# Slots of the timetable set anew in a relative-position attention layer with a ternary feed-forward

## The reference

```python
idx = clip(r[None, :] - r[:, None], -64, 64) + 64
h = layernorm(x)
q, k, v = proj(h, Wq, bq), proj(h, Wk, bk), proj(h, Wv, bv)          # (8, 16, 1024, 16)
logits = einsum('bhqd,bhkd->bhqk', q, k) + einsum('bhqd,qkd->bhqk', q, embK[idx])
w = softmax(logits)
out = einsum('bhqk,bhkd->bhqd', w, v) + einsum('bhqk,qkd->bhqd', w, embV[idx])
x = x + layernorm(out.reshape(8, 1024, 256) @ Wo.T + bo)
delta = 0.7 * mean(abs(Wf))
Wt = where(Wf > delta, 1, where(Wf < -delta, -1, 0)) * alpha
x = x + layernorm(layernorm(x) @ Wt.T + bf)
```

## Time and profile before

| | |
|---|---|
| median of 3 runs | 2754.64 us (2754.41 to 2755.69) |
| the profiled execution | 2754.83 us |
| its span, first to last instruction | 2753.0 us |
| mean granted clock of PE | 0.98 of 2.4 GHz |
| busy: PE, DVE, ACT, POOL | 94%, 74%, 56%, 35% |
| transfers | 409.11 MB, mean 149 GB/s |

### The profile page before, as it was taken

How to read it: one execution, slowest core, us unless ns; L and a number is a source line. 1 busy time by engine, 2 the same in 40 slices (tenths; PEclk the granted TensorE clock), 3 DMA queues, 4 the chain that set the end, 5 groups by cost and what they waited for, 6 DMA issues and landing times.

```text
span 2753.0 us, 102969 instructions
## 1 busy us (share of the span) xinstructions
PE 2594.8 (94%) x43410; PEld 1969.1 (72%) x43410; DVE 2033.1 (74%) x5187; ACT 1552.1 (56%) x2993; POOL 956.8 (35%) x2275
## 2 busy tenths in 40 slices
PE   5899999999999999999999999999999999999995
PEld 3577777677777777767777777767777677777773
DVE  3777678777886778866788667877678766887775
ACT  2455566556565555555555565555665556566651
POOL 3114323433344333443244332444323433341026
PEclk8799999999999999999999999999999999999997
DMA  7656655456455564555645556446655457445410
GB/s 220 182 140 181 166 150 144 121 168 190 126 153 136 154 181 139 143 147 156 173 129 155 160 156 168 131 127 180 169 150 141 115 169 195 137 137 152 131 43 28
DMA packets 605048, 409.11 MB, mean 149 GB/s; under 512 B 149162, under 2 KB 604330, under 8 KB 604330
## 3 DMA queue, kind: packets, MB, share of 16 engines
q1 hardware_dynamic: 604586, 402.54, 51.7%
HBM read 206.84 MB, written 194.90 MB: 146 GB/s over the span
## 4 chain that ended last, share of the span: by engine, by line
PE 70%; DVE 15%; issue 4%; POOL 4%; ACT 3%; SPq 1%; DMA 1%; DVEq 0%; POOLq 0%; ACTq 0%
PE oacc L797 16%; PE logitsT L759 15%; PE scores L736 15%; PE logitsT L764 7%; DVE maxes L1016 6%; DVE junk L1013 6%; PE misc L860 4%; PE misc L693 4%; ACT wxr L1216 2%; PE misc L822 2%; POOL rs L1249 2%; PE misc L710 2%; PE misc L810 2%; PE misc L834 2%; POOL rs L1254 1%
## 5 line engine op out<-in xcount | busy, mean ns | idle before, releaser
L1013 DVE CUSTOM_DVE_ANT_1 junk<-scores,bands 128x512 bf16<-128x512 f32 x988 | 679.1, 687 | 490.8 <-PE scores L736 470.5
L759 PE MATMUL logitsT<-qs,ks 98*128 98x128 bf16 (+3 forms) x9088 | 995.0, 216 | 21.5 <-ACT wxr L1216 12.4
L1216 ACT ACTIVATE wxr<-logitsT 128x512 f32<-128x512 f32 x1024 | 588.6, 603 | 527.6 <-PE logitsT L759 437.5
L759 PEld LDWEIGHTS logitsT<-qs,ks 98*128 98x128 bf16 (+1 forms) x9088 | 678.7, 99 | 244.2 <-issue 90.4
L1216 ACT ACTIVATE wy<-logitsT 128x512 f32<-128x512 f32 x1024 | 585.1, 596 | 408.8 <-PE logitsT L759 395.2
L736 PE MATMUL scores<-ks,qs 101*128 101x256 bf16 (+10 forms) x4096 | 716.9, 291 | 62.8 <-DVE maxes L1016 33.7
L1016 DVE TENSOR_REDUCE maxes<-scores 128x1 f32<-128x512 f32 x1024 | 701.7, 685 | 2.6 <-PE scores L736 2.6
L736 PEld LDWEIGHTS scores<-ks,qs 96*128 96x128 bf16 (+3 forms) x4096 | 302.4, 100 | 243.1 <-DVE maxes L1016 110.9
L764 PE MATMUL logitsT<-ident,bands 128*128 128x128 f32 x2048 | 468.2, 280 | 0.0
L1244 POOL TENSOR_SCALAR rs<-rs 128x1 int32<-128x1 int32 (+1 forms) x224 | 43.4, 194 | 871.3 <-DVE rs L924 860.6
L764 PEld LDWEIGHTS logitsT<-ident,bands 128*128 128x128 f32 x2048 | 292.5, 143 | 34.2 <-issue 0.2
(11 more groups left out here) (136 smaller groups left out, 2570.2 us busy)
## 6 DMA issues: line engine op xcount, KB each, us to landing
bs<-praw SPq DMA_DIRECT2D x256, 512.0 KB, 4.5
bands<-bs SPq DMA_DIRECT2D x224, 512.0 KB, 4.3
ks<-kd SPq DMA_DIRECT2D x64, 384.0 KB, 5.0
qs<-qd SPq DMA_DIRECT2D x112, 192.0 KB
bands<-bs SPq DMA_DIRECT2D x128, 128.0 KB, 3.7
qd<-qparts SPq DMA_DIRECT2D x64, 192.0 KB, 2.9
kd<-kparts SPq DMA_DIRECT2D x64, 192.0 KB, 2.6
qd<-qparts SPq DMA_DIRECT2D x64, 128.0 KB, 2.4
```

The costliest lines, as they stand in the source:

```text
L759: mm = e.matmul(lt[:, c * P + q0:c * P + q1], kk[0:depth, h, kt * P:(kt + 1) * P], qs[i][0:depth, h, q0:q1], start=q0 == 0, stop=not near, ...
L1013: e.tensor_tensor_reduce(junk[:], scores[:, 0:512].rearrange("p (a c) -> p a c", a=2), banded, 1.0, LOWEST, ALU.add, ALU.max, mx[:, h, 0:1 ...
L1216: e.activation(dst, src, ACT.Exp).then_inc(exp_ready, 1)
```

## The change

Slots and lags are set anew; no instruction is added, taken away or altered. The parts:

- `tail_normed` on DVE from o + 8.2 to o + 8.6 (slot 6.2 to 5.4, lag 2.0 to 3.2); `tail_x1T` on PE from o + 10.5 to 9.6 and on ACT from 10.7 to 9.6; `tail_wo` 0.2 later, `tail_out` on DVE 0.3 later, `tail_store` 0.8 later.
- the last four tiles: spacing 1.05 to 0.85, `tail_attT` 0 to 0.3, `tail_out` 6.5 to 7, `tail_load` 4 slots later.
- `band_read` of block 1 two slots earlier; `merge` 0.3 earlier; `max_reduce` 0.1 later, `max_rows` 0.2 earlier; `out_copy` 0.1 earlier, `relative` 0.1 later.
- projections of batches 1 to 7: `turn_x` 0.1 later (on ACT 0.2 earlier), `project_q` 0.3 later (on ACT 0.8 later), `project_k` 0.2 earlier.
- the start: `ternary` from slot 8 to 4, `reltab` 4 later, `load_k` of the first keys, `statistics`, `normalise`, `project_v` and the first `band_raw`.

```diff
-        at(2 + 2.5 * i, "reltab", i)
+        at(6 + 2.5 * i, "reltab", i)
...
-    at(8, "ternary")
+    at(4, "ternary")
...
-                at(0.1 * c - (102.4 if c else 110), "statistics", b, c)
-                late = (((4, "project_q"), (4.8, "far"), (1.3, "project_k"), (2.9, "project_v"), (8.5, "write_q"),
+                at(0.2 * c - (102.4 if c else 110), "statistics", b, c)
+                late = (((4, "project_q"), (4.8, "far"), (1.3, "project_k"), (3, "project_v"), (8.5, "write_q"),
...
-                        ((1.3, "project_q"), (3.4, "far"), (5.2, "project_k"), (5.8, "project_v"), (6, "write_q"),
+                        ((1.3, "project_q"), (3.4, "far"), (5.2, "project_k"), (5.6, "project_v"), (6, "write_q"),
...
-                for x, stage in ((-9.5 if c else -3, "normalise"), (0, "turn_x")) + late:
+                for x, stage in ((-9.5 if c else -3.3, "normalise"), (0, "turn_x")) + late:
...
-                for x, stage in ((-7, "load_x"), (-5.2, "statistics"), (-2.6, "normalise"), (0, "turn_x"), (1, "project_q"),
-                                 (2.1, "project_v"), (4, "far"), (6.5, "write_q"), (10.2, "project_k"),
+                for x, stage in ((-7, "load_x"), (-5.2, "statistics"), (-2.6, "normalise"), (0.1, "turn_x"), (1.3, "project_q"),
+                                 (2.1, "project_v"), (4, "far"), (6.5, "write_q"), (10, "project_k"),
...
-                at(z - 41.8 + 8 * c if n else 10.2 * c - (92.5 if keys_first(0, c) else 88), "load_k", n, c)
+                at(z - 41.8 + 8 * c if n else 10.1 * c - (92.5 if keys_first(0, c) else 84), "load_k", n, c)
...
-        r0 = m0 if s else -55
+        r0 = m0 if s else -54.7
...
-            at(r0 - 9 + 4 * blk, "band_read", s, blk)
+            at(r0 - 9 + 2 * blk, "band_read", s, blk)
...
-        at(m0 + 6.4, "max_reduce", s)
-        at(m0 + 7.5, "max_rows", s)
+        at(m0 + 6.5, "max_reduce", s)
+        at(m0 + 7.3, "max_rows", s)
...
-            at(o + 3.5, "merge", s, blk)
+            at(o + 3.2, "merge", s, blk)
         if i % 2:
-            at(w0 + 7.7, "out_copy", s // 2)
+            at(w0 + 7.6, "out_copy", s // 2)
...
-                    at(z + 29.6 + 1.5 * part + 0.35 * piece, "relative", quad, part, piece)
+                    at(z + 29.7 + 1.5 * part + 0.35 * piece, "relative", quad, part, piece)
...
-                at(z + 26 + i, "tail_load", b, t)
-                for x, stage in ((0, "tail_attT"), (0.41, "tail_wo"), (2.07, "tail_x1"), (2.4, "tail_norm"),
-                                 (3.9, "tail_normed"), (4.3, "tail_x1T"), (4.7, "tail_ff"), (6.5, "tail_out"),
+                at(z + 30 + i, "tail_load", b, t)
+                for x, stage in ((0.3, "tail_attT"), (0.41, "tail_wo"), (2.07, "tail_x1"), (2.4, "tail_norm"),
+                                 (3.9, "tail_normed"), (4.3, "tail_x1T"), (4.7, "tail_ff"), (7, "tail_out"),
                                  (6.8, "tail_store")):
-                    at(z + 36.6 + 1.05 * i + x, stage, b, t)
+                    at(z + 36.6 + 0.85 * i + x, stage, b, t)
...
-            for x, stage in ((-1, "tail_load"), (0, "tail_attT"), (0.8, "tail_wo"), (3, "tail_x1"), (4, "tail_norm"),
-                             (6.2, "tail_normed"), (10.5, "tail_x1T"), (11.3, "tail_ff"), (13.5, "tail_out"),
-                             (14.99, "tail_store")):
+            for x, stage in ((-1, "tail_load"), (0, "tail_attT"), (1, "tail_wo"), (3, "tail_x1"), (4, "tail_norm"),
+                             (5.4, "tail_normed"), (9.6, "tail_x1T"), (11.3, "tail_ff"), (13.5, "tail_out"),
+                             (15.79, "tail_store")):
...
-            "tail_wo": 0.9, "tail_x1": 1.0, "tail_norm": 1.4, "tail_normed": 2.0, "tail_ff": 0, "tail_out": 1.6},
-    "ACT": {"turn_x": 0.3, "far": 0.9, "project_q": 0.7, "project_k": 0, "band_raw": 0.25, "tail_attT": 0, "tail_x1T": 0.2},
+            "tail_wo": 0.9, "tail_x1": 1.0, "tail_norm": 1.4, "tail_normed": 3.2, "tail_ff": 0, "tail_out": 1.9},
+    "ACT": {"turn_x": 0, "far": 0.9, "project_q": 1.2, "project_k": 0, "band_raw": 0.25, "tail_attT": 0, "tail_x1T": 0},
```

## The result

The changed kernel takes 2712.36 us (median of 4 runs, 2709.06 to 2715.24) where the kernel before, run beside it, takes 2754.52 (2752.28 to 2755.69): a ratio of 0.9847, 95% interval 0.983 to 0.9865. That is 42 us faster. The profiled execution took 2711.58 us.

The account below looks back on a forecast made before the run. PE, busy 94%, was taken to lose time at six stalls for DVE and the clock falls behind them; -11.1 - 9.0 - 1.0 + 2.0 + 0.4 - 0.4 = -19.1 us gave 2735.7, range 2727 to 2748 (0.85).

Parts of the forecast that it names:

- the stalls: PE's six waits for DVE's L1013 in tile 7 of batches 0 to 5, one of 1.59 and five of 1.90 us.
- the 3.3 us less between the same points of two batches: Sign that the forecast is right: in steady work each batch is 3.3 us shorter.
- `tail_normed` on DVE, -11.1 us: Tile 7: with L1117 behind head 5's `row_max`, PE's whole L1013 stall goes, six times; bounds -11.1 and 0.
- the clock, -9.0 us: Behind the six stalls the clock no longer falls to 1.2 GHz: 1.5 us times six, bounds -10.2 and 0.
- 0.1 at most: Tile 7 of batch 1: PE's remaining wait at the next scores, at 844.07, after `tail_normed` moves.
- The same goes for `max_rows`, `max_reduce`, `out_copy`, `turn_x`, `project_q` and `project_k`: These stages move 0.8 slots at most, PE finds its inputs there and ACT is half idle: taken as 0.
- I put this at 0: Tails: `tail_x1T` comes closer behind L1117, but a margin of some 0.5 to 1.3 us hides it: 0.
- rival 3: PE waits at x1T for L1117 in 60 tiles; at 0.6 us each 36 us, time 2772; chance 0.07.
- `merge` and `relative`, -1.0 us with bounds of -3 and +2: Earlier merge ends L810's weight-load waits, 12.8 us, mostly beside matmuls, but delays hand-overs of `scores` by up to 0.7 us.
- Rival 4: More is won: earlier merges and bands also take a quarter of L1016's 29.8 us; time 2728.3; chance 0.12.
- Rival 2: The stalls go but the clock still falls, so 9.0 us less is won; time 2744.7; chance 0.13.
- `ternary`, first keys, last tiles: +2.0, +0.4, -0.4 us: Start and end: PE waits again for L1013, `load_k` 2 delays `load_k` 3, tile 3's `tail_ff` may find its bank sooner.

## Why the prediction was wrong

The direction, the stalls and the clock behind them were forecast rightly. The size failed at the steps that took moves within PE's order as worth nothing. Of the signs that were named, the waits and the clock came as said; the 3.3 us less between the same points of two batches came out as 6.1 (42.89 over the seven batches of the stretch).

- **`tail_normed` on DVE, -11.1 us, and the clock, -9.0 us: right in mechanism, and about right in size.** Taken out of the changed kernel it costs 20.9 us of the stretch, where the two terms say 20.1; that five falls and not six came back, two of them twice as long, makes the closeness partly luck. L1013 keeps 2.4 us of waits, and a fall of the clock costs 1.3 to 1.6 us where I took 1.5. In the kernel before it gave only 14.7 us: L683 waited 2.5 us more for POOL, L797 stood 1.3 us more, and the clock gave less than 9.0. In the changed kernel the waits of L683 are 0.3 us. The "0.1 at most" that I left for PE at the next scores is 0.63 in tile 7 of batch 1. No wait of L1117 for POOL is left, as forecast.
- **"The same goes for `max_rows`, `max_reduce`, `out_copy`, `turn_x`, `project_q` and `project_k`: they move by 0.8 slots at most, on a PE that finds its inputs there": this step failed.** The slots of the projections are worth 13.1 us in the changed kernel and 16.8 in the kernel before. (Of the 16.8, one fall of the clock is some 1.6.) I asked whether the moved stage finds its inputs, and took its place in PE's order as free. It is not, for two reasons that the runs show. Between two heads of `scores` that stand close, its matmuls give DVE time to catch up; the run with `project_k` alone shows this at one place, 0.21 us of 0.45, and 5.6 of the 13.1 us stand at L736. And the same matmuls take more or less time by what stands beside them: L693's eight from 1.92 down to 1.72 us, 3.3 of the 13.1 us, with no wait in the rows; the cause of this is open. How the rest comes about, 4.2 us with one fall of the clock among it, is not shown. The lags of ACT are worth 2.9 us alone, of which one fall of the clock is some 1.6.
- **`tail_x1T` and `tail_wo`, "I put this at 0": failed in the same way.** They are worth 7.9 us of the stretch in the changed kernel, won at the hand-overs of `scores`. I looked for a loss there (rival 3) and not for a gain. Rival 3 did not come.
- **`merge` and `relative`, -1.0 us with bounds of -3 and +2.** All step edits together, with `band_read` and the maxima, are worth 0.6 us or nothing in the changed kernel, in the range. Both effects that I named, the end of L810's waits and the later hand-overs, are seen in the weight loads' rows, 13.1 and 8.8 us; in PE's time they hardly show, so that the sum is in the range does not prove the reason. Alone in the kernel before the two gave 8.1 us; some 3.2 of that is the clock, the other 4.9 lie outside the bounds.
- **Rival 4, "a quarter of the 29.8 us of L1016's hand-overs", 2728.3 us, was the nearest.** It named the right wait but took it from earlier merges and bands. The rows of L1016 fall by 6.5 us only. The change takes 22 us beside the stalls and the clock. Much of that lies within groups of matmuls: L736's groups take 12.2 us less, of which the run with `tail_normed` alone has 1.1. A bound from PE's rows of waits was therefore no bound.
- **Rival 2, the clock falls all the same: wrong.** With the stalls gone there is no fall in the stretch, neither here nor in the kernel before plus `tail_normed`. By the rule of the Trainium skill that the prediction weighed ("TensorE: Matmul & The Clock Gate", "HAM oscillation — how this bites in real kernels") the falls, which it puts down to longer idle stretches, would have stayed; the trace does not agree.
- **`ternary`, first keys, last tiles: +2.0, +0.4, -0.4 us.** Without the start edits the time is 2714.34 us, without those of the last tiles 2709.06. As the same kernel comes to step 8 up to 4 us apart, these terms can't be told from 0. L674 ran at 106.99 us with a wait of 1.55, as foreseen, but the wait of 1 to 2 us behind it is not a steady loss: at step 8 the changed kernel was 0.2 us behind in one profile and 2.2 ahead in the other. From the first of the last 13 roots to the end it takes 41.7 us, and 41.5 before: the same length, as forecast.

The waits of PE's weight loads for the halves of `scores`, over 300 to 2600 us, say more of what was there to be won. In the kernel before they are

```profile
PEld scores L736 <- DVE maxes L1016: 92.3, 227, 0.9
PEld scores L736 <- DVE maxes L1013: 26.7, 64, 2.1
```

and in the changed one

```profile
PEld scores L736 <- DVE maxes L1016: 78.2, 198, 0.5
PEld scores L736 <- DVE maxes L1013: 19.9, 76, 0.8
```

Together these are 119.0 us and 98.1. Part of such a wait lies beside a running matmul, so they say too much, as PE's own rows, 42.5 us for the same two waits, say too little. Nor do they hold the whole gain: with the projections' slots alone they fell from 119.0 to 113.4 us while the stretch won 16.8.

## What to carry to other kernels

Where one engine fills a buffer of two halves and another empties it at nearly the same rate, all other work of the first is padding, and a hand-over profits from having some in front of it. Cost the move of any stage, even one whose inputs have long been there, by the gaps that it opens and closes between the hand-overs, and do not take its own length as fixed: it can change with its neighbours (1.92 and 1.72 us here). Read waits in the durations of groups too (0.85 us for a group that takes 0.61 elsewhere) and in the rows of the weight loads, since rows of waits alone miss what is waited for within a group. And measure a part by taking it out of the finished kernel as well: alone, the parts gave 14.7, 19.1, 11.0 and 9.8 us in the stretch, 54.6 together, where the whole gave 42.9, mostly because together they saved 14 falls of the clock where there were six to save.

## What the runs showed of the hardware

**The same stall does not always lower the clock.** The kernels that kept the six stalls of 1.6 to 2.1 us had from 2 to 6 falls to 1.2 GHz in steady work: over nine of them, 39 falls behind 54 stalls. Four of the 39 lasted twice as long as the others. Nor does a fall need one of these stalls: without the projections' slots the changed kernel has one behind L797's wait of 1.55 us, shown above. The two stalls of 1.59 and 1.58 us shown above, with the same instructions around them, came out differently. So a gain in one such kernel can be the clock's and not the edit's, by some 1.3 to 1.6 us a fall. What decides it is open.

**The middle of a run repeats far better than its ends.** Two profiles of the changed kernel agree to 0.11 us over 2261 us, and differ by 2.3 us in the 240 us before. Two of the one less the step edits differ by 0.6 and by 4.0 us.

**The same matmuls take different times beside different neighbours.** The eight matmuls of L693 took 1.92 us from their start to that of the next group ahead of L797, and 1.72 us behind L736 and ahead of L759, with no wait in PE's rows at either place. Why is open.
